# Attention with one more whole-array product per pair of heads in the narrow key blocks

## The chip, the cores and the metric

The kernel runs on one core of a Trainium2 chip. The time is the device time of that core in microseconds (us). The kernel before took 4295.83 us, the median of three runs (4293.31 to 4297.06).

## The reference

Two layers are computed for a batch of 2 sequences of 1024 tokens with 512 features. The change is in the attention of the first:

```python
q = (x @ Wq.T + bq).reshape(b, l, h, hd).transpose(0, 2, 1, 3)      # k and v alike; h = 32, hd = 16
scores = jnp.einsum('bhqd,bhkd->bhqk', q, k) / math.sqrt(hd)
causal = jnp.tril(jnp.ones((l, l), bool))
scores = jnp.where(causal, scores, -jnp.inf)
att = jax.nn.softmax(scores, axis=-1)
out = jnp.einsum('bhqk,bhkd->bhqd', att, v)
out = out.transpose(0, 2, 1, 3).reshape(b, l, d)
return out @ Wo.T + bo
...
x = x + _layernorm(_L0_attn_ref(_layernorm(x, axis=-1), ...), axis=-1)
x = x + _layernorm(_L0_ffn_ref(...), axis=-1)       # low-rank weight factors, silu
x = x + _layernorm(_L1_attn_ref(...), axis=-1)      # a state-space (Mamba) layer
x = x + _layernorm(_L1_ffn_ref(...), axis=-1)
```

## The kernel before, in words

A loop over the two batches runs every layer in turn. Each engine has its own program, and all follow one list, `ORDER`, made by `attention_order()`, so the order of work is written out by hand. Semaphores join the engines.

Attention works on eight groups of four heads, `t` = 0 to 7, here called quads. Queries and keys of a head are stacked as high and low parts in 48 rows (`ROWS`), with two rows more for the row maxima. An even quad has its rows from partition 0 on and an odd quad from partition 64 on.

A quad has twelve steps (`STEPS`), here called blocks 0 to 11. A block is one half `s` of the queries (512 of them) against one block `j` of 128 keys. Blocks 0 to 3 are the first half and blocks 4 to 11 the second. Since the attention is causal, blocks 1, 2, 3 and 9, 10, 11 are narrow: `lo` is 128, 256 and 384, and only 384, 256 or 128 queries are left. The other six blocks have 512.

In each block TensorE makes, for each of the four heads, a score product (L652) into `bank[h]`, and between them "pieces" (L628): the score products of the next quad with queries and keys exchanged, from which VectorE (DVE) takes the row maxima (L1237 with the mask, L1242 without). The pieces use a ring of three banks (4, 5, 7), and TensorE waits for `ring_free` before each. After the score products come the value products of the block before (`values`, L671), four heads side by side in the columns of the array. ScalarE (ACT) takes the exponential of two heads at once (L948, 384 of them), and TensorE waits for `exp_done[h // 2]` before it writes these two banks again. GpSimd (POOL) masks the diagonal block (L1608). The value products wait for that. The last block of a half ends in a copy `ot` on DVE (L1264), which is turned by four transposes (L681, "turn") in block 1 of the next quad and in block 7. Quad 7 has no pieces, because no quad follows it.

The query and key projections of later quads (L492, L493, L494: products over all 128 rows and columns) stand in blocks 1, 3, 5 and 7 of quads 1 and 3, twelve of them at a time. `xhi`, the input of the layer in its rounded form, stays in place until the attention has ended.

Of the kernel before, what the change touches and what calls it, by code (L numbers as in the profile page):

```python
# [24 lines left out]
P = 128  # L25
TT = L // P
KT = D // P
HALF = 512
# [35 lines left out]
def build(nc, x, w_attn, qk_bias, bv, bo, w_ffn0, lr0, lr0_const, w_ffn1,  # L64
          w_mamba, w_dt, conv_par, dt_bias, a_log, d_skip, out):
    ctx = ExitStack()
    with ctx:
        def sb(name, shape, dt=F32, stack=ctx):
            return stack.enter_context(nc.sbuf_tensor(name, shape, dt))
# [5 lines left out]
        bank = [banks[:, i, :] for i in range(8)]  # L75
# [4 lines left out]
        xhi = sb("xhi", [P, KT, L], F32R)  # L80
# [406 lines left out]
        def _(pe):  # L487
# [8 lines left out]
            def tokens(dst, i, w_hi, w_lo, cols=None):  # L496

                tok = slice(i * P, (i + 1) * P)
                for kt in range(KT):
                    r = three(dst, lambda k: xhi[:, k, tok], lambda k: xlo[:, k, tok],  # L500
                              lambda k: w_hi[:, k, :], lambda k: w_lo[:, k, :], kt, kt == 0, kt == KT - 1)
                return r

            def features(dst, w_hi, w_lo, s):

                tok = slice(s * HALF, (s + 1) * HALF)
                for kt in range(KT):
                    r = three(dst, lambda k: w_hi[:, k * P:(k + 1) * P], lambda k: w_lo[:, k * P:(k + 1) * P],
                              lambda k: xhi[:, k, tok], lambda k: xlo[:, k, tok], kt, kt == 0, kt == KT - 1)
                return r  # L510
# [85 lines left out]
            with pe.Fori(0, B) as b:  # L596
# [5 lines left out]
                for what, *arg in ORDER:  # L602
                    if what == "proj":
                        f, use = arg
                        which = use // 2
                        if use == 0:
                            pe.wait_ge(wqk_ready, b * 8 + 2 * f + 2)
                        if ring >= 3:
                            pe.wait_ge(ring_free, b * RING + ring - 2)
                        features(bank[RING_BANKS[ring % 3]][:], wqk_hi[:, which, :], wqk_lo[:, which, :], use % 2  # L610
                                 ).then_inc(ring_done, 1)
                        ring += 1
                    elif what == "values_in":
                        i, = arg
                        if i == 0:
                            pe.wait_ge(wv_ready, b + 1)
                        pe.wait_ge(ring_free, b * RING + ring - 2)
                        tokens(bank[RING_BANKS[ring % 3]][:], i, wv_hi, wv_lo).then_inc(ring_done, 1)
                        ring += 1
                    elif what == "piece":  # L620
                        t, n = arg
                        h, i, s, cols, _ = PIECES[n]
                        base, buf = 64 * (t % 2), t // 2 % 2
                        if n == 0:
                            pe.wait_ge(stacked[t % 2], (b * (NQ // 2) + t // 2 + 1) * STACKED)
                        pe.wait_ge(ring_free, b * RING + ring - 2)
                        dst = bank[RING_BANKS[ring % 3]]
                        r = pe.matmul(dst[:, 0:cols], stack_q[buf][base:base + ROWS, h, i * P:(i + 1) * P],  # L628
                                      stack_k[buf][base:base + ROWS, h, s * HALF:s * HALF + cols],
                                      start=True, stop=True)  # L630
                        r.then_inc(ring_done, 1)
                        ring += 1
                    elif what == "maxima":
                        t, = arg
                        pe.wait_ge(mx_ready, b * NQ + t + 1)
                        pe.wait_ge(ring_free, b * RING + ring - 2)
                        pe.transpose(bank[RING_BANKS[ring % 3]][0:QUAD * TT, 0:P], mx[:, 0, :], ident[:]
                                     ).then_inc(ring_done, 1)
                        ring += 1
                    elif what == "score":  # L640
                        t, n, h = arg
                        s, j = STEPS[n]
                        lo = max(j * P - s * HALF, 0)
                        base, buf = 64 * (t % 2), t // 2 % 2
                        it = b * (NQ * NS) + (t * NS + n)
                        if n == 0 and h == 0 and t % 2 == 0 and t < 4:
                            pe.wait_ge(ones_rows, b * (16 * 8) + 16 * 4 * (t // 2 + 1))
                        if n == 0 and h == 0:
                            pe.wait_ge(mt_in, START + (b * NQ + t + 1) * 32)
                        if h % 2 == 0:  # L650
                            pe.wait_ge(exp_done[h // 2], START + it)
                        r = pe.matmul(bank[h][:, 0:HALF - lo],  # L652
                                      stack_k[buf][base:base + ROWS + 2, h, j * P:(j + 1) * P],
                                      stack_q[buf][base:base + ROWS + 2, h, s * HALF + lo:(s + 1) * HALF],
                                      start=True, stop=True)
                        if h % 2:
                            r.then_inc(st_done[h // 2], 1)
                    elif what == "values":
                        t, n = arg
                        s, j = STEPS[n]  # L660
                        lo = max(j * P - s * HALF, 0)
                        it = b * (NQ * NS) + (t * NS + n)
                        if j == 0:
                            pe.wait_ge(ot_ready, START + b * (2 * NQ) + 2 * t + s)
                        for p in range(2):
                            if j * P >= s * HALF:
                                pe.wait_ge(masked[p], b * (NQ * TT) + (t * TT + j + 1))
                            else:
                                pe.wait_ge(exp_done[p], START + it + 1)
                        for h in range(QUAD):  # L670
                            r = pe.matmul(bank[6][32 * h:32 * h + VW, lo:HALF], V[:, j, QUAD * t + h, :],  # L671
                                          probs[n % 2][:, h, 0:HALF - lo], start=j == 0,
                                          stop=j == CPH * (s + 1) - 1, skip_group_check=True,
                                          tile_position=(0, 32 * h))
                        r.then_inc(pv_done, 1)
                    elif what == "turn":
                        t, s = arg
                        pe.wait_ge(ot_ready, START + b * (2 * NQ) + 2 * t + s + 1)
                        pe.wait_ge(ring_free, b * RING + ring - 2)
                        for k in range(CPH):  # L680
                            r = pe.transpose(bank[RING_BANKS[ring % 3]][:, k * P:(k + 1) * P], ot[:, k * P:(k + 1) * P], ident[:])  # L681
                        r.then_inc(ring_done, 1)
                        ring += 1
# [1104 lines left out]
```

## Time and profile before

| | us |
|---|---|
| median of the runs | 4295.83 |
| the profiled execution, its own time | 4294.83 |
| its span, from the first to the last instruction | 4293.1 |
| attention of the first batch, block 0 of quad 0 to the last value products | 347.27 |
| mean granted clock of TensorE over the span | 0.907 |

The clock is given as a share of full speed: 1.00 is 2.4 GHz and 0.50 is 1.2 GHz. A mean between them is a mixture of the two levels. In a row of the timeline the start of one product and the start of the next tell what the first one costs. The duration includes a pipeline that overlaps the next.

### The profile page before, as it was taken

How to read it: one execution, taken by the hardware profiler on the slowest of the kernel's cores; microseconds unless marked ns; L12 is line 12 of the kernel's file. 1: busy time of each engine (PE TensorE's matmuls, PEld its weight loads, DVE VectorE, ACT ScalarE, POOL GpSimd, SP SyncE). 2: the span in 40 equal slices, each digit the busy share in tenths (PEclk: the TensorE clock that was granted, in tenths of full speed). 3: DMA queues.
4: the chain of work that ended last, by engine and by line, in shares of the span. 5: the costliest groups of instructions: out<-in, count | busy, mean ns of one | idle time of the engine just before them, and what ended most of it. 6: DMA issues, size and time to landing. Idle time of an engine off the chain costs nothing.

```text
span 4293.1 us, 61464 instructions
## 1 busy us (share of the span) xinstructions
PE 3861.4 (90%) x18056; PEld 2813.5 (66%) x18056; DVE 2711.2 (63%) x5034; ACT 1695.2 (39%) x3538; POOL 1880.8 (44%) x2017
## 2 busy tenths in 40 slices
PE   7899799689999999979878896996899999999797
PEld 4444478567777777757654444885677777777576
DVE  3567445577777777764435673555777777777644
ACT  1344411355545555541113444113555555555411
POOL 1111344355555655654311113443555556655542
PEclk8677899899999999989977767998999999999899
DMA  3221011011100111001032210110101001110010
GB/s 73 36 36 31 24 51 45 22 33 30 32 20 25 34 32 29 22 15 45 35 81 36 36 32 29 46 45 22 35 28 32 20 25 34 32 29 22 15 52 35
DMA packets 81456, 145.59 MB, mean 34 GB/s; under 512 B 16392, under 2 KB 18520, under 8 KB 81264
## 3 DMA queue, kind: packets, MB, share of 16 engines
q1 hardware_dynamic: 81264, 143.28, 12.9%
q8 instruction: 90, 1.47, 0.1%
q14 instruction: 102, 0.84, 0.1%
HBM read 113.08 MB, written 4.19 MB: 27 GB/s over the span
## 4 chain that ended last, share of the span: by engine, by line
PE 69%; issue 11%; DVE 7%; ACT 4%; POOL 3%; DVEq 2%; POOLq 2%; DMA 1%; SPq 1%; ACTq 0%
PE banks L492 15%; PE banks L493 14%; PE banks L494 14%; PE banks L832 4%; PE banks L671 4%; PE banks L652 3%; PE banks L628 3%; PE banks L825 2%; PE banks L845 2%; DVE conv L1344 2%; DVEq L1347 1%; PE banks L767 1%; PE banks L768 1%; POOL X L1509 1%; ACT conv L1005 1%
## 5 line engine op out<-in xcount | busy, mean ns | idle before, releaser
L1344 DVE SCALAR_TENSOR_TENSOR conv<-banks,cpar,conv 128x509 f32<-128x509 f32 (+2 forms) x576 | 428.2, 744 | 115.3 <-ACT conv L1005 100.9
L948 ACT ACTIVATE probs<-banks 128x1024 f32<-128x1024 f32 (+3 forms) x384 | 297.7, 810 | 309.4 <-PE banks L652 308.9
L1172 DVE TENSOR_TENSOR Y<-banks,Y 128x512 f32<-128x512 f32 x400 | 276.1, 691 | 188.1 <-PE banks L494 187.9
L1608 POOL TENSOR_SCALAR_AFFINE_SELECT probs<-probs 128x256 f32<-128x256 f32 x256 | 104.2, 408 | 645.8 <-ACT probs L948 645.5
L628 PE MATMUL banks<-stack_k,stack_q 48*128 48x512 f32 (+3 forms) x768 | 331.7, 502 | 59.3 <-DVEq L1218 19.8
L1672 POOL TENSOR_TENSOR state<-state,gt 128x512 f32<-128x512 f32 x112 | 133.5, 1192 | 500.4 <-PE banks L825 500.4
L492 PE MATMUL banks<-xhi,f_hi 128*128 128x512 f32 x800 | 322.6, 403 | 3.5 <-DVE xlo L1143 3.5
L492 PE MATMUL banks<-xhi,wx_hi 128*128 128x512 f32 x768 | 312.0, 406 | 14.4 <-DVE conv L1344 14.4
L493 PE MATMUL banks<-xhi,f_lo 128*128 128x512 f32 x800 | 319.9, 400 | 0.0
L494 PE MATMUL banks<-xlo,f_hi 128*128 128x512 f32 x800 | 319.4, 399 | 0.0
L494 PE MATMUL banks<-xlo,wx_hi 128*128 128x512 f32 x768 | 306.0, 398 | 0.0
L493 PE MATMUL banks<-xhi,wx_lo 128*128 128x512 f32 x768 | 306.0, 398 | 0.0
L1237 DVE CUSTOM_DVE_ANT_0 banks<-banks,mask_qk 128x128 f32<-128x128 f32 (+3 forms) x512 | 248.1, 500 | 72.7 <-PE banks L628 59.4
L832 PEld LDWEIGHTS banks<-xdt,decay 128*128 128x128 f32 x2048 | 248.5, 192 | 65.2 <-issue 65.2
L652 PE MATMUL banks<-stack_q,stack_k 50*128 50x512 f32 (+3 forms) x768 | 274.7, 459 | 5.2 <-ACT probs L948 2.9
L628 PEld LDWEIGHTS banks<-stack_k,stack_q 48*128 48x128 f32 x768 | 163.0, 235 | 157.9 <-DVE mx L1242 51.1
L492 PE MATMUL banks<-wg_hi,xhi 128*128 128x512 f32 x512 | 222.3, 434 | 45.5 <-DVE conv L1344 42.2
L652 PEld LDWEIGHTS banks<-stack_q,stack_k 50*128 50x128 f32 x768 | 157.0, 232 | 155.5 <-issue 116.8
L832 PE MATMUL banks<-xdt,decay 128*128 128x64 f32 x2048 | 242.7, 272 | 2.4 <-DVE decay L1363 2.4
L910 ACT CAST h_hi<-hf 128x512 fp32r<-128x512 f32 x100 | 62.2, 622 | 441.0 <-DVE hf L1161 441.0
L518 PE MATMUL banks<-ident,xn 128*128 128x128 f32 x256 | 66.5, 426 | 188.1 <-ACT xn L892 165.3
L1076 ACT ACTIVATE yv<-banks,gt 128x64 f32<-128x64 f32 x1024 | 223.8, 332 | 24.8 <-PE banks L825 24.8
(209 smaller groups left out, 10185.0 us busy)
## 6 DMA issues: line engine op xcount, KB each, us to landing
m_raw<-in_w_mamba SPq DMA_DIRECT2D x224, 256.0 KB, 2.6
f_raw<-in_w_ffn SPq DMA_DIRECT2D x50, 768.0 KB, 4.5
stack_q<-part_hi SPq DMA_DIRECT2D x128, 64.0 KB, 2.4
stack_k<-part_hi SPq DMA_DIRECT2D x128, 64.0 KB, 2.5
X<-in_x SPq DMA_DIRECT2D x4, 1024.0 KB, 6.5
wqk_raw<-in_w_attn SPq DMA_DIRECT2D x8, 512.0 KB, 3.5
stack_q<-part_lo SPq DMA_DIRECT2D x64, 64.0 KB, 2.4
stack_k<-part_lo SPq DMA_DIRECT2D x64, 64.0 KB, 2.5
```

Source lines behind the costliest of these rows:

```text
L492: pe.matmul(dst, a_hi(kt), w_hi(kt), start=first, stop=False)
L493: pe.matmul(dst, a_lo(kt), w_hi(kt), start=False, stop=False)
L494: return pe.matmul(dst, a_hi(kt), w_lo(kt), start=False, stop=last)
L628: r = pe.matmul(dst[:, 0:cols], stack_q[buf][base:base + ROWS, h, i * P:(i + 1) * P], stack_k[buf][base:base + ROWS, h, s * HALF:s * HALF ...
L652: r = pe.matmul(bank[h][:, 0:HALF - lo], stack_k[buf][base:base + ROWS + 2, h, j * P:(j + 1) * P], stack_q[buf][base:base + ROWS + 2, h, s ...
L671: r = pe.matmul(bank[6][32 * h:32 * h + VW, lo:HALF], V[:, j, QUAD * t + h, :], probs[n % 2][:, h, 0:HALF - lo], start=j == 0, stop=j == C ...
L832: r = pe.matmul(bank[7][:, h * MP:(h + 1) * MP], decay[:, h, :], xdt[:, h * MP:(h + 1) * MP], start=True, stop=True, skip_group_check=True)
L948: act.activation(probs[n % 2][:, 2 * p:2 * p + 2, 0:w], banks[:, 2 * p:2 * p + 2, 0:w], ACT.Exp, scale=1.0 / HD ** 0.5).then_inc(exp_done[ ...
L1076: r = act.activation(yv[:, own], bank[6][:, own], ACT.Identity, scale=gt[:, EC, c, h:h + 1])
L1172: dve.tensor_tensor(Y[:, i, :], bank[6 + i % 2], Y[:, i, :], ALU.add).then_inc(f["dn_used"], 1)
L1237: dve.tensor_tensor_reduce(out=src, in0=src, in1=mask_qk[:, HALF - cols:HALF], scale=1.0, scalar=NEG, op0=ALU.add, op1=ALU.max, accum_out= ...
L1344: r = dve.scalar_tensor_tensor(out=rest, in0=src[:, 0:HALF - lag], scalar=cpar[:, o:o + 1], in1=rest, op0=ALU.mult, op1=ALU.add)
```

## The change

In a narrow block a product over the whole array, 128 rows and 128 columns by 512, is issued before the scores of heads 0 and 2. Its operands are two slices of `xhi`. It writes all of `bank[h]`, and the score product of that head overwrites it. Nothing reads its result.

```diff
                         if h % 2 == 0:
                             pe.wait_ge(exp_done[h // 2], START + it)
+                        if lo and h % 2 == 0:
+                            pe.matmul(bank[h][:], xhi[:, 0, 0:P], xhi[:, 0, 0:HALF], start=True, stop=True)
                         r = pe.matmul(bank[h][:, 0:HALF - lo],
                                       stack_k[buf][base:base + ROWS + 2, h, j * P:(j + 1) * P],
                                       stack_q[buf][base:base + ROWS + 2, h, s * HALF + lo:(s + 1) * HALF],
                                       start=True, stop=True)
```

In TensorE's program before, block 11 of quad 3 (128 queries left) up to its first value products reads as follows. `stack_q, stack_k` are scores and `stack_k, stack_q` are pieces.

```order
L651 REGISTER_ALU
L652 MATMUL banks<-stack_q,stack_k 128x128
L626 REGISTER_ALU
L628 MATMUL banks<-stack_k,stack_q 128x384
L652 MATMUL banks<-stack_q,stack_k 128x128
L626 REGISTER_ALU
L628 MATMUL banks<-stack_k,stack_q 128x512
L652 MATMUL banks<-stack_q,stack_k 128x128
```

The same place now. L653 is the new line, and the lines behind it have moved by two.

```order
L651 REGISTER_ALU
L653 MATMUL banks<-xhi 128x512
L654 MATMUL banks<-stack_q,stack_k 128x128
L626 REGISTER_ALU
L628 MATMUL banks<-stack_k,stack_q 128x384
L654 MATMUL banks<-stack_q,stack_k 128x128
L626 REGISTER_ALU
L628 MATMUL banks<-stack_k,stack_q 128x512
L653 MATMUL banks<-xhi 128x512
L654 MATMUL banks<-stack_q,stack_k 128x128
```

The first new product stands ahead of the first score product, the second between a piece and the third score product. Each takes over the wait for `exp_done`. There are 96 of them in the program of a batch, 192 in all. Nothing else on TensorE moves, and the other engines' programs are as they were.

## Rows read from the trace of the kernel before

**Rows 1.** The page: busy time of the engines, and TensorE's clock in 40 slices.

```profile
PE 3861.4 (90%) x18056; PEld 2813.5 (66%) x18056; DVE 2711.2 (63%) x5034; ACT 1695.2 (39%) x3538; POOL 1880.8 (44%) x2017
...
PEclk8677899899999999989977767998999999999899
```

**Rows 2.** Windows, with their columns: the first batch's attention, and 26 us of it.

```profile
core 0: us, PE busy (x) PEld busy (x) DVE busy (x) ACT busy (x) POOL busy (x), PEclk, DMA share, GB/s
127.23:474.50 347.27, 322.68 (x1645) 149.45 (x1645) 204.42 (x626) 154.04 (x200) 65.33 (x134) 0.74 0.20 36
370.00:396.00 26.00, 25.93 (x113) 10.82 (x114) 15.96 (x52) 9.91 (x13) 2.04 (x5) 0.50 0.00 1
```

**Rows 3.** Timeline of TensorE: start, us, engine, line, product; quad 4 to quad 5.

```profile
405.98 1.19 PE L671 MATMUL banks<-probs,V 128*17 128x256 f32 x16
407.11 0.49 PE L652 MATMUL banks<-stack_q,stack_k 50*128 50x512 f32 x1
...
408.95 0.44 PE L652 MATMUL banks<-stack_q,stack_k 50*128 50x384 f32 x1
...
411.09 1.91 PE L671 MATMUL banks<-probs,V 128*17 128x512 f32 x8
```

**Rows 4.** Windows: blocks 1 to 3 of quads 0, 1, 2, 3, 5 and 7.

```profile
129.56:141.46 11.90, 11.82 (x52) 4.54 (x52) 8.46 (x26) 4.45 (x7) 3.27 (x8) 0.50 0.70 106
169.91:195.67 25.76, 22.33 (x79) 11.92 (x80) 9.86 (x29) 4.97 (x8) 6.63 (x10) 0.60 0.00 1
230.38:241.98 11.60, 10.76 (x55) 4.20 (x54) 9.12 (x28) 4.34 (x7) 3.27 (x8) 0.74 0.68 102
271.67:294.92 23.25, 19.99 (x79) 10.19 (x79) 9.91 (x29) 4.98 (x8) 6.63 (x10) 0.71 0.00 1
367.56:380.68 13.12, 13.01 (x55) 4.95 (x54) 9.25 (x28) 4.34 (x7) 3.27 (x8) 0.56 0.00 1
449.54:457.09 7.55, 6.97 (x41) 3.04 (x41) 0.68 (x2) 4.12 (x7) 2.89 (x8) 0.77 0.27 96
```

**Rows 5.** Windows: blocks 4 to 8 of quads 0, 2, 4, 5 and 7.

```profile
141.46:160.10 18.64, 18.55 (x88) 8.33 (x85) 11.55 (x38) 9.69 (x10) 0.41 (x1) 0.57 0.61 99
241.98:261.74 19.76, 19.76 (x89) 8.98 (x86) 11.72 (x38) 9.69 (x10) 0.82 (x2) 0.50 0.60 98
341.19:357.93 16.74, 16.65 (x88) 7.30 (x84) 11.46 (x38) 9.69 (x10) 0.41 (x1) 0.68 0.63 103
380.68:399.30 18.62, 18.52 (x89) 8.27 (x85) 11.55 (x38) 9.69 (x10) 0.41 (x1) 0.58 0.00 1
457.09:468.60 11.51, 11.01 (x68) 4.25 (x64) 1.37 (x3) 9.02 (x10) 6.95 (x4) 1.00 0.00 0
```

**Rows 6.** Windows: blocks 9 to 11 of quad 4, and of quad 7 nearly to its end.

```profile
399.30:407.11 7.81, 7.07 (x59) 3.48 (x56) 6.02 (x20) 3.48 (x6) 2.86 (x7) 1.00 0.03 6
468.60:473.80 5.20, 4.89 (x40) 2.10 (x36) 0.00 (x0) 3.86 (x7) 2.74 (x8) 1.00 0.00 0
```

**Rows 7.** Timeline of TensorE: projection products at both clocks, then the scores.

```profile
303.47 0.63 PE L494 MATMUL banks<-xlo,wqk_hi 128*128 128x512 f32 x1
303.90 0.56 PE L492 MATMUL banks<-xhi,wqk_hi 128*128 128x512 f32 x1
...
305.70 0.40 PE L493 MATMUL banks<-xhi,wqk_lo 128*128 128x512 f32 x1
305.93 0.39 PE L494 MATMUL banks<-xlo,wqk_hi 128*128 128x512 f32 x1
306.25 0.50 PE L652 MATMUL banks<-stack_q,stack_k 50*128 50x512 f32 x1
...
306.59 0.62 PE L652 MATMUL banks<-stack_q,stack_k 50*128 50x512 f32 x2
```

**Rows 8.** Timeline of TensorE: pieces that wait for VectorE, in blocks 9 and 11.

```profile
400.58 0.50 PE L628 MATMUL banks<-stack_k,stack_q 48*128 48x512 f32 x1 [0.30 <-DVE mx L1242]
...
405.73 0.18 PEld L628 LDWEIGHTS banks<-stack_k,stack_q 48*128 48x128 f32 x1 [0.38 <-DVE mx L1237]
```

## The prediction, as put on record before the changed kernel ran

> **What bounds the kernel now.** I read the page first. TensorE is busy for 90% of the span, more than any other engine, and the row of its clock shows two dips. They lie in slices 2 to 6 and 22 to 25, where the two batches do their attention [rows 1]. Next I read the windows. The attention of the first batch takes 347.27 us at a mean clock of 0.74, with TensorE busy for 93% of it and VectorE for 59% [rows 2]. The second row says more: in 26 us TensorE is busy for 25.93 and the clock is 0.50 all along. So the clock is low where the engine is not idle at all. What it does there are score products and pieces of 50 and 48 rows and value products, with turns in between. The stretches at 1.00 follow the projections or a turn.
>
> The reader should then look at where the clock falls. In quad 4 it is 1.00 in blocks 9 to 11 [rows 6]. Then a double set of value products ends at 407.2 (405.98 plus 1.19), and until 411.09 there is nothing but scores and pieces: block 0 and then block 1 [rows 3]. The clock falls in that stretch. In nearly all quads the fall comes at this place. It rises again in block 1 or 2 in some quads (mean clock of blocks 1 to 3: 0.74 in quad 2, and quad 4 is like it) and in others only in block 7, when the turn is made (0.56 in quad 5, and quad 6 is like it) [rows 4]. Blocks 4 to 8 are mostly at 0.50: 18.64, 19.76 and 18.62 us, and 16.74 at 0.68 in quad 4, against 11.51 in quad 7, which has no pieces [rows 5].
>
> At the high clock the bound is another one. In blocks 9 to 11 of quad 4 VectorE is busy for 6.02 of 7.81 us and TensorE for 7.07 [rows 6], and pieces wait 0.30 and 0.38 us for the maxima [rows 8]. In blocks 1 to 3 VectorE needs 9.25 us at whatever clock [rows 4]. That is the floor there.
>
> **The change, part by part.** It adds 192 products: 2 in each of 6 blocks, 8 quads, 2 batches. It removes and moves nothing. Each takes over a wait that the score product had, so behind it in TensorE's queue stand that score product and all else of the block. ScalarE waits for them, and after it POOL's mask and the value products.
>
> *The price of one.* Inside a train of whole-array products one costs 0.23 us at the high clock (305.70 to 305.93) and 0.43 at the low one (303.47 to 303.90) [rows 7]. But these stand alone among products of another shape. After the last of a train the first score product comes 0.32 us later and the next pair another 0.34, where the plain spacing is 0.23 to 0.24: some 0.19 more for going over [rows 7]. I take 0.42 at the high clock. The lower end is 0.23, and nothing where all is covered. At the low clock I take 0.60, with 0.43 and 0.80 as the ends, since there the same detour costs up to twice as much. The Trainium skill (TensorEngine Tiling (Array Packing), Key Properties) says that changing the tiling mode drains TensorE. The trace agrees as far as the 0.19 us go. Without that rule the price would be 0.23 and the term of blocks 9 to 11 about half.
>
> *Blocks 9 to 11*, which run at 1.00 already. Nothing can be gained there. Six products of 0.42 are 2.5 us per quad. TensorE's idle 0.74 us (7.81 less 7.07) and the wait for the maxima hide about 1.0 of it [rows 6, 8], so 1.5 us remain in quads 0 to 6 of both batches: 14 × 1.5 = 21. In quad 7 there is no VectorE work to hide behind, the blocks take 5.20 us with TensorE busy for 4.89 [rows 6], and I count 2.3 for each: 4.6. Together **+25 us**. The ends are 5 (all covered) and 35.
>
> *Blocks 1 to 3.* The two products of block 1 fall into the stretch of rows 3, and those of blocks 9 to 11 move block 0 later by 1.5 us against the points at which the clock is set. Projections, which are products of the same kind, hold or restore the clock in quads 1 and 3. So I expect that some falls do not come, and that after others the clock is back by the turn in block 1. A quad without projections can go three ways. Without a fall the blocks cost VectorE's 9.25 plus 1.5 as above: 10.7 us. With a fall and an early rise they cost 12. Staying low they cost 13.1 plus six times 0.60: 16.7. I weigh these 0.5, 0.35 and 0.15, which gives 12.1. Against before that is −1.0 in quads 5 and 6 and +0.5 in quads 2 and 4 (11.60) [rows 4]. Quad 0 starts at the low clock and has no turn: 11.9 becomes 12.9. Quads 1 and 3 took 25.76 at clock 0.60 and 23.25 at 0.71, so 0.11 of clock is worth 2.5 us [rows 4]. With the clock at 0.8 and 0.85, and 0.9 for the products, they come to 22 and 21: −3.8 and −2.3. Quad 7, with 7.55 and no VectorE cover, pays 2.5 and gets 1.2 back: +1.3. The sum is −2.0 + 1.0 + 1.0 − 6.1 + 1.3 = −4.8 per batch, so **−10 us**. The ends are −36 (no falls: 9 to 18 per batch, see below) and +58 (96 × 0.60).
>
> *Blocks 4 to 8.* They get no product. When the clock is high at the end of block 3 it may last into block 4 or 5 before it falls. A block costs 4.0 us low and 2.8 high (18.62 for five, the last of them at the high clock; 7.81 for three narrow ones) [rows 5, 6]. Half a block saved in five quads of each batch is 0.6 × 10: **−6 us**. The ends are 0 and −44.
>
> The sum is 25 − 10 − 6 = +9 us on the profiled execution's 4294.83, so 4303.8. The median of the runs lies 1.0 higher, so I predict **4305 us**. A measurement of this kernel can tell a change of 0.2% (8.6 us) from none, so the forecast sits just at that bound.
>
> **The rivals.**
>
> *The clock is held through blocks 0 to 3 in every quad.* For it speaks that whole-array products do keep the clock in quads 1 and 3. Against it speaks that block 0, where the bare stretch begins, gets none, and that two products are little beside twelve. Blocks 1 to 3 would take 10.7 in five quads and 19, 18.5 and 8.3 in quads 1, 3 and 7: 99.3 against 117.7 before, −18 per batch. With +25 and −6 that gives 4295.83 − 17 = 4279.
>
> *It is then held through blocks 4 to 8 too.* They would take 5 × 2.8 = 14 us instead of 18.64, 19.76, 16.74 and twice 18.6: −22 per batch. Quad 7 runs these blocks at 1.00 throughout [rows 5], and quads 1 and 3 do it in part. Against it: block 4 has nothing but the shortest value products (128 queries) between scores and pieces, as barren a stretch as block 0. The time would be 4295.83 + 25 − 36 − 44 = 4241.
>
> *Slower: bought at the low clock.* The mechanism is that the two products of a block are too few to move a rise or a fall, and blocks 1 to 3 pay the price at 0.50. The price is 0.60 × 96 = 58 us, less what projections give back in quads 1 and 3, with 25 in blocks 9 to 11 on top: 4295.83 + 45 + 25 = 4366 at the full price, and 4340 if VectorE still hides a part. It decides if the mean clock of blocks 1 to 3 in quads 5 and 6 stays below about 0.7. For it speaks that TensorE is never idle there, so every product shows in full.
>
> *TensorE's busy time decides the clock.* The Trainium skill (TensorE: Matmul & The Clock Gate, Part 1) says that the clock follows how busy the engine has recently been. Rows 2 contradict the plain reading of that: busy for 25.93 of 26 us at 0.50. As a mechanism of this kernel it would leave the clock as it is, since the engine is busy already. The time is then that of the slower rival, and its chance is in that one's.
>
> *The products cost nothing and do nothing*, because waits for VectorE and ScalarE hide them. Idle time of TensorE is 25 us in the first attention (347.27 less 322.68) [rows 2], which is no more than a part of what they take. That would be 4298.
>
> **How the numbers follow.** Forecast 0.45, with its own range 4285 to 4325. The clock held in blocks 0 to 3: 0.18. Held further: 0.10. Bought at the low clock: 0.20. Nothing: 0.07. The likeliest gives 4305. The range of 8 in 10 leaves out most of the second rival below and the dear half of the third above: 4256 to 4350. Slower by over 0.2% is half of the forecast (0.22), the third rival (0.20) and a bit more: 0.45. Faster is the first two rivals and a sixth of the forecast: 0.35. The rest is 0.20.
>
> **What would show it.** In the windows of the changed kernel, blocks 9 to 11 of quads 0 to 6 should be 1.5 us longer at clock 1.00. Blocks 1 to 3 of quads 5 and 6 should have a mean clock of about 0.8 and last 12 us. The new line should have 192 products. A product should delay its neighbours by 0.4 us. The forecast is wrong if blocks 4 to 8 come down from 18.6 to near 14 us (then the clock is held), if blocks 1 to 3 grow by more than 2 us (then it was bought at the low clock), or if the narrow blocks at 1.00 grow by less than 0.5 us (then the price is hidden).

## The result, and the profile after

The changed kernel takes 4338.26 us (median of nine runs, 4325.41 to 4361.07) against 4297.06 us of the kernel before in the same comparison (nine runs, 4290.15 to 4315.62). The ratio is 1.0103, with a 95% interval of 1.0079 to 1.0127: slower by 1.0%. The direction was forecast and the time lies in the range, but the loss is 41 us where I had forecast 9.

The profiled execution took 4358.16 us, near the upper end of its kernel's runs, and its span is 63.2 us longer than before. That is 22 us more than the medians differ, so the two traces show more of a loss than the kernels usually have. The page, answering to [rows 1], shows the 192 products more, TensorE busy for 68 us more, and the other engines as they were.

```profile
PE 3929.1 (90%) x18248; PEld 2839.6 (65%) x18248; DVE 2711.8 (62%) x5034; ACT 1699.0 (39%) x3538; POOL 1877.9 (43%) x2017
```

The windows of the changed kernel follow, the ones that answer to [rows 2, 4]: the attention of the first batch, blocks 1 to 3 of its quads 0, 1, 2, 3, 5 and 7, and the attention of the second batch.

```profile
core 0: us, PE busy (x) PEld busy (x) DVE busy (x) ACT busy (x) POOL busy (x), PEclk, DMA share, GB/s
128.99:499.92 370.93, 348.69 (x1733) 158.96 (x1733) 204.31 (x626) 156.14 (x200) 64.94 (x134) 0.79 0.19 33
132.04:146.80 14.76, 14.76 (x57) 5.43 (x57) 7.97 (x25) 3.72 (x7) 2.85 (x7) 0.50 0.65 106
177.41:204.34 26.93, 22.64 (x84) 12.37 (x83) 9.50 (x29) 4.70 (x8) 6.29 (x10) 0.68 0.00 1
241.33:251.16 9.83, 9.63 (x61) 4.29 (x60) 8.05 (x27) 4.03 (x7) 2.94 (x8) 1.00 0.63 103
289.48:310.93 21.45, 18.27 (x84) 9.37 (x84) 9.05 (x27) 4.41 (x8) 6.21 (x9) 0.85 0.00 1
382.96:394.28 11.32, 11.25 (x62) 4.85 (x61) 7.94 (x27) 4.01 (x7) 2.90 (x8) 0.85 0.01 2
461.40:474.56 13.16, 13.16 (x47) 5.64 (x46) 0.68 (x2) 3.73 (x7) 2.78 (x7) 0.50 0.03 13
...
2301.89:2675.19 373.30, 350.67 (x1729) 159.73 (x1733) 204.57 (x626) 155.83 (x199) 64.76 (x133) 0.79 0.19 33
```

The mean clock of the first attention rose from 0.74 to 0.79, and the attention is 24 us longer all the same. Quads 2 and 5 got what was hoped for: 11.60 us became 9.83 and 13.12 became 11.32. Quad 7 went from 7.55 at 0.77 to 13.16 at 0.50.

Next, to be read against [rows 5, 6], blocks 4 to 8 of quads 2, 4 and 7, and blocks 9 to 11 of quads 2 and 4:

```profile
251.16:271.17 20.01, 19.48 (x90) 8.08 (x86) 12.30 (x40) 9.62 (x10) 0.81 (x2) 0.59 0.60 96
357.23:371.42 14.19, 13.48 (x89) 5.53 (x85) 11.89 (x40) 9.62 (x10) 0.79 (x3) 1.00 0.64 103
474.56:492.51 17.95, 17.95 (x70) 7.11 (x66) 1.37 (x3) 9.53 (x10) 6.88 (x4) 0.56 0.00 1
271.17:286.42 15.25, 15.25 (x62) 6.61 (x62) 6.50 (x20) 3.59 (x6) 2.44 (x6) 0.50 0.02 4
371.42:380.69 9.27, 8.80 (x62) 4.23 (x62) 6.07 (x20) 3.58 (x6) 2.48 (x7) 1.00 0.26 46
```

In quad 4 the clock was held through blocks 4 to 8: 14.19 us against 16.74 [rows 5]. In quad 2 it fell early in these blocks and did not come back within the quad, and blocks 9 to 11 took 15.25 us at 0.50, where before they took 8.09 at 0.90. In quad 7 blocks 4 to 8 took 17.95 against 11.51.

Such windows over all quads of both batches account for the attention (us, sum of both batches):

| | before | after | change | forecast |
|---|---|---|---|---|
| blocks 9 to 11 | 121.1 | 158.8 | +37.7 | +25 |
| blocks 0 to 3 | 267.1 | 275.9 | +8.8 | −10 |
| blocks 4 to 8 | 300.3 | 309.5 | +9.3 | −6 |
| of all these, quad 7 | 53.3 | 84.3 | +31.0 | +7 |

That is 55.8 of the 63.2 us. The rest lies around the attentions. The first product of block 1 is issued before that block's first score and so falls into the window of block 0, and that of block 9 into the window of blocks 4 to 8. Blocks 1 to 3 alone are 1 us shorter than before, and block 0 is 10 us longer over the sixteen quads.

### The profile page after: what moved, and what is told of

It reads as the page before. It is cut to its first block, busy times and chain, and to the rows that moved or that the text cites. A ratio compares the mean times of both kernels' runs of the same rounds, so it can differ in the third digit from the quotient of the medians.

```text
span 4356.3 us, 61848 instructions
## 1 busy us (share of the span) xinstructions
PE 3929.1 (90%) x18248; PEld 2839.6 (65%) x18248; DVE 2711.8 (62%) x5034; ACT 1699.0 (39%) x3538; POOL 1877.9 (43%) x2017
## 3 DMA queue, kind: packets, MB, share of 16 engines
q1 hardware_dynamic: 81264, 143.28, 12.6%
## 4 chain that ended last, share of the span: by engine, by line
PE 71%; issue 11%; DVE 7%; ACT 4%; POOL 3%; DVEq 2%; POOLq 2%; SPq 1%; DMA 0%; ACTq 0%
PE banks L492 15%; PE banks L493 14%; PE banks L494 14%; PE banks L834 4%; PE banks L673 4%; PE banks L654 4%; PE banks L628 3%; PE banks L827 2%; PE banks L653 2%; PE banks L847 2%; DVE conv L1346 2%; DVEq L1349 1%; PE banks L769 1%; PE banks L770 1%; POOL X L1511 1%
## 5 line engine op out<-in xcount | busy, mean ns | idle before, releaser
L628 PE MATMUL banks<-stack_k,stack_q 48*128 48x512 f32 (+3 forms) x768 | 306.3, 464 | 52.4 <-DVEq L1220 18.7
L1492 POOL TENSOR_SCALAR f_hi<-f_raw 128x512 fp32r<-128x512 f32 x150 | 95.8, 639 | 312.9 <-PE banks L494 293.8
```

## The experiments

In each kernel only the condition or the body of the two new lines differs. The kernel before was timed beside each group on the same chip, so the ratio is what counts, and not the distance to a time that I expected: its own median was 4298.83, 4302.77 and 4307.06 us in the three groups. As a measure of the clock I also give its mean over blocks 1 to 3 of quads 4, 5 and 6 of both batches, six windows of one profiled execution each. One trace is one sample: in several of them the two batches have the same pattern nearly window for window. It is 0.58 in the kernel before and 0.88 in the changed one.

**Blocks 1 to 3 only.**

```diff
-                        if lo and h % 2 == 0:
+                        if lo and s == 0 and h % 2 == 0:
```

> The added products stand only in blocks 1 to 3 (96 of the 192), the other narrow blocks are as before. My theory (the products act on TensorE's clock, and where the clock is high they cost 0.4 us each): blocks 9 to 11 with block 0 shrink from 11.5 to 9.7 us per quad, blocks 1 to 3 of quads 4 to 6 stay at 10 to 12 us, the time is about 4308 (4290 to 4325). The rival (the products only take TensorE time, the clock follows other things): half of the loss goes, 4317, and the clock in blocks 1 to 3 of quads 5 and 6 is as before, 0.54 to 0.56.

Measured: 4306.09 us (12 runs), ratio 1.0023 (1.0006 to 1.0040). The clock measure is 0.94. The trace is of the fastest of the twelve (4283.64), so it shows the best case. The rows are blocks 1 to 3 of quad 6, blocks 9 to 11 of quad 5 and, in the second batch, blocks 4 to 8 of quad 5.

```profile
408.31:418.00 9.69, 9.66 (x62) 4.27 (x61) 7.91 (x27) 4.01 (x7) 2.91 (x8) 1.00 0.00 0
...
398.25:406.04 7.79, 7.06 (x60) 3.48 (x56) 6.00 (x20) 3.48 (x6) 2.84 (x7) 1.00 0.03 8
...
2522.24:2536.00 13.76, 13.04 (x88) 5.34 (x84) 11.88 (x40) 9.63 (x10) 0.43 (x2) 1.00 0.00 1
```

As expected, the price in blocks 9 to 11 is gone (7.79 against 9.27 us) and the clock is held in the first half. Quads 4, 5 and 6 of the second batch ran from block 1 to block 8 at 1.00, 23.4 us each, where the same three took 28.8 to 29.5 before. The rival's clock of 0.54 to 0.56 did not come. Without the other half of the products three quarters of the changed kernel's loss are gone.

**Blocks 9 to 11 only.**

```diff
-                        if lo and h % 2 == 0:
+                        if lo and s == 1 and h % 2 == 0:
```

> The added products stand only in blocks 9 to 11 (96 of the 192). My theory: these blocks run at the high clock already, so nothing is gained; they pay 1.9 us per quad, 30 us in all, and block 0 only comes later against the points at which the clock is set; blocks 1 to 3 are as before, 13 us in quads 5 and 6. The time is 4325 (4310 to 4340). The rival (price only, half of it): 4317.

Measured: 4335.27 us (6 runs), ratio 1.0095 (1.0076 to 1.0115), clock measure 0.61. The rows are blocks 4 to 8 of quad 7 in the first batch, and blocks 1 to 3 and 9 to 11 of quad 5 in the second.

```profile
458.56:478.25 19.69, 19.69 (x69) 7.49 (x65) 1.38 (x3) 9.69 (x10) 7.30 (x5) 0.50 0.00 1
2543.15:2556.14 12.99, 12.92 (x54) 5.21 (x54) 8.88 (x28) 4.45 (x7) 3.25 (x8) 0.50 0.00 1
2572.16:2581.41 9.25, 8.78 (x61) 4.24 (x61) 6.07 (x20) 3.59 (x6) 2.47 (x7) 1.00 0.03 7
```

This half alone brings nearly the whole loss, 0.95% of 1.03%. Blocks 9 to 11 are 28 us longer than before over both batches (9 of them in quad 7), with no return, and quad 7 was at the low clock though its blocks 1 to 3 had no products.

**No products in quad 7.**

```diff
-                        if lo and h % 2 == 0:
+                        if lo and t + 1 < NQ and h % 2 == 0:
```

> The changed kernel without the added products in quad 7 (168 are left). My theory: the loss in quad 7 (blocks 1 to 8 went from 19 to 31 us in the first batch, at the low clock) is partly the products there; without them blocks 1 to 8 go back to about 20 us, and the time falls by 25 to 4313. The rival (price only): 24 products by 0.42 us, so 4328. A third case: quad 7 stays at the low clock since the clock depends on when it starts, then about 4325 with blocks 4 to 8 of quad 7 still near 18 us.

Measured: 4337.08 us (10 runs), ratio 1.0071 (1.0047 to 1.0095). Four runs lie at 4308.5 to 4313.1 and six at 4336.3 to 4341.6, with none between. The trace is of one at 4310. Its rows are blocks 1 to 3 and 4 to 8 of quad 7, first in batch one and then in batch two.

```profile
452.05:461.37 9.32, 9.12 (x41) 3.82 (x41) 0.68 (x2) 4.22 (x7) 3.18 (x8) 0.52 0.14 52
461.37:478.53 17.16, 17.16 (x68) 6.68 (x65) 1.38 (x3) 9.10 (x10) 6.62 (x4) 0.56 0.00 1
2608.10:2615.67 7.57, 6.99 (x40) 3.06 (x40) 0.68 (x2) 4.12 (x7) 2.87 (x8) 0.77 0.16 60
2615.67:2627.18 11.51, 11.00 (x68) 4.26 (x64) 1.37 (x3) 9.00 (x10) 6.91 (x4) 1.00 0.01 1
```

The third case holds for the first batch. With not one product in it, quad 7 took 7.4 us longer there in these blocks than in the second batch of the same execution, plain instructions against plain instructions. My 4313 was wrong as a median. The two traces also give the price at the low clock: the changed kernel's blocks 1 to 3 (13.16 us) have five whole products more than these 9.32, so 0.77 each where nothing covers them. In quad 0, also at the low clock, five products made 11.90 us into 14.76, which is 0.57 each.

**The score product twice instead of a whole-array product.**

```diff
-                            pe.matmul(bank[h][:], xhi[:, 0, 0:P], xhi[:, 0, 0:HALF], start=True, stop=True)
+                            pe.matmul(bank[h][:], stack_k[buf][base:base + ROWS + 2, h, j * P:(j + 1) * P],
+                                      stack_q[buf][base:base + ROWS + 2, h, s * HALF:(s + 1) * HALF],
+                                      start=True, stop=True)
```

> Instead of the product over the whole array the score product itself is made once more, 50 rows by 128 columns by 512, same places and number, so TensorE streams the same number of elements with no change of the array's shape. My theory (it is the whole array that holds the clock): the clock is as in the kernel before, 0.54 to 0.56 in blocks 1 to 3 of quads 5 and 6, which last 13.1 plus 6 times 0.43 = 15.7 us; the time is 4340 (4325 to 4360). The rival (any product holds it): clock of blocks 1 to 3 of quads 4 to 6 at 0.85 to 1.0 and 10 to 11.5 us as in the changed kernel, time 4320 as the price is smaller.

Measured: 4327.16 us (6 runs), ratio 1.0069 (1.0053 to 1.0086), clock measure 0.72. The rows are blocks 9 to 11 of quad 5, blocks 1 to 3 of quad 6 (both of the first batch), and blocks 1 to 3 of quad 4 in the second.

```profile
403.98:412.31 8.33, 7.93 (x62) 4.29 (x59) 6.05 (x20) 3.48 (x6) 2.57 (x7) 1.00 0.03 8
414.49:427.87 13.38, 13.31 (x61) 6.28 (x59) 8.98 (x28) 4.11 (x7) 3.02 (x8) 0.51 0.01 1
2493.65:2503.00 9.35, 8.56 (x60) 4.16 (x57) 7.88 (x27) 4.12 (x7) 3.03 (x8) 1.00 0.62 103
```

The price is 0.5 us for blocks 9 to 11 instead of 1.5. The array's shape does not change, and some of the products run beside a piece: the one that starts at 403.64 us has a piece starting at 403.65. How much of the difference each of these makes was not separated. The clock is between the two theories: as without products in two quads of the first batch, held in one of the second. One trace can't decide it, for reasons that the later runs show. What stands is that 50 rows held it in fewer places than 128 did in any of the five traces with two whole-array products in each of blocks 1 to 3 only or of all narrow blocks there (0.72 against 0.88 to 0.96). The time lost is less all the same, 0.7% against the changed kernel's 1.0%.

**Blocks 1 to 3 of quads 2, 4, 5 and 6.**

```diff
-                        if lo and h % 2 == 0:
+                        if lo and s == 0 and t in (2, 4, 5, 6) and h % 2 == 0:
```

> The added products stand only in blocks 1 to 3 of quads 2, 4, 5 and 6 (48 of the 192). My theory: these are the places where they turn low clock into high and nothing else needs their time; against the version with products in blocks 1 to 3 of all quads (4306) quads 0, 3 and 7 save 3.6, 3.6 and 2.7 us per batch, so about 4286, faster than the kernel before by 0.3% (4270 to 4300). Blocks 4 to 8 of quads 4 to 6 at a clock of 0.9 to 1.0 and 14 to 15 us. The rival (the clock is a matter of chance and the products do not steer it): the clock of these quads is as in the kernel before, 0.5 to 0.7 in blocks 1 to 8, and the time is 4299 plus 48 by 0.5 = 4323.

Measured: 4289.59 us (12 runs, 4272.61 to 4310.03), ratio 0.9966 (0.9944 to 0.9989): the only version faster than the kernel before. The clock measure is 0.96. The rows are blocks 1 to 3 and 4 to 8 of quad 4, blocks 4 to 8 of quad 7, and in the second batch blocks 9 to 11 of quad 3.

```profile
327.93:337.59 9.66, 9.64 (x62) 4.27 (x61) 7.91 (x27) 4.01 (x7) 2.90 (x8) 1.00 0.64 105
337.59:351.36 13.77, 13.07 (x88) 5.34 (x84) 11.88 (x40) 9.63 (x10) 0.43 (x2) 1.00 0.60 98
436.95:454.30 17.35, 17.35 (x69) 6.80 (x65) 1.38 (x3) 9.10 (x10) 6.64 (x4) 0.56 0.00 1
2452.57:2464.29 11.72, 11.72 (x60) 5.70 (x56) 6.20 (x20) 3.47 (x6) 2.45 (x7) 0.50 0.12 20
```

The clock was up through blocks 1 to 8 in seven of the eight quads with products (mean 0.85 and more), and these eight are 36 us shorter than in the trace before. But 31 us of it are lost in the other quads of this trace. Quad 7 lies low in both batches (+20 us), and quad 3 of the second batch fell after its projections and took 11.72 us for blocks that take 7.8 (+10 for the quad). The eighth, quad 4 of the second batch, comes right behind it and starts at the low clock.

**Two products in blocks 0, 1, 4 and 5.**

```diff
-                        if lo and h % 2 == 0:
+                        if n in (0, 1, 4, 5) and t + 1 < NQ and h % 2 == 0:
```

> The added products (two per block) stand in blocks 0, 1, 4 and 5 of quads 0 to 6, where the clock is seen to fall, instead of the narrow blocks (112 products). My theory (a fall comes where scores and pieces run for long with hardly any value products): the clock stays at 1.00 from block 4 on in most quads without projections, blocks 4 to 8 take 14 to 15 us with part of the products hidden behind VectorE, 9 to 11 are 7.8; the time is 4290 (4270 to 4310). The rival (place does not matter, only the number of products): about as the changed kernel scaled to 112 of 192 products, 4320, with low stretches in blocks 4 to 8 as before.

Measured: 4350.73 us (6 runs), ratio 1.0095 (1.0066 to 1.0124), clock measure 0.79: my expectation of 4290 failed by 60 us. The rows are blocks 1 to 3 and 4 to 8 of quad 4, and 4 to 8 of quad 5.

```profile
342.22:356.54 14.32, 14.25 (x57) 5.41 (x57) 8.68 (x27) 3.99 (x7) 2.85 (x7) 0.50 0.63 102
356.54:374.61 18.07, 17.98 (x88) 6.92 (x87) 11.61 (x37) 9.91 (x10) 0.41 (x1) 0.72 0.31 52
394.72:408.88 14.16, 13.97 (x90) 5.58 (x89) 11.56 (x39) 9.91 (x10) 0.41 (x1) 1.00 0.00 1
```

Quad 5 went as I thought and most others did not: blocks 4 to 8 were at a clock of 0.55 to 0.72 in five of six windows of quads 4 to 6, and the products there were paid at the low clock. So filling the places where the fall is seen is not enough. That blocks 2 and 3, which have little of everything, have to be filled too is my reading. This run left 6 to 11 bare as well, and can't tell them apart.

**Two products in every block of quads 0 to 6.**

```diff
-                        if lo and h % 2 == 0:
+                        if t + 1 < NQ and h % 2 == 0:
```

> Two added products in every block of quads 0 to 6 (168). If the clock can be held by such products at all, it is 1.00 nearly throughout quads 2, 4, 5 and 6 once it has risen. The price is 24 products per quad by 0.42 us, partly hidden: quads 4 to 6 take 36 to 38 us each against 41 before and 33.5 with products in blocks 1 to 3 and a held clock. Time 4320 (4300 to 4345). The rival (they only take time): 4299 + 168 by 0.45 = 4375.

Measured: 4335.28 us (10 runs), ratio 1.0071 (1.0049 to 1.0093), clock measure 0.92. The rows are blocks 4 to 8 of quad 4 and block 0 and blocks 1 to 3 of quad 5.

```profile
362.81:378.65 15.84, 15.84 (x96) 6.25 (x95) 11.82 (x39) 10.25 (x10) 0.54 (x2) 1.00 0.60 96
388.64:392.38 3.74, 3.74 (x11) 1.57 (x10) 1.95 (x6) 1.64 (x2) 0.41 (x1) 0.50 0.02 4
392.38:404.99 12.61, 12.60 (x61) 5.34 (x61) 8.55 (x26) 3.99 (x7) 2.84 (x7) 0.77 0.00 1
```

Blocks 4 to 8 ran at 1.00 in quads 1 to 6 of both batches, and TensorE is then busy for 15.84 of 15.84 us. So the clock can be held there, and 2.1 us a quad is what it costs against 13.77. Even so the clock still fell ahead of block 0 of quad 5 in both batches, and with a price in every block the kernel is 0.7% slower. The rival's 4375 is excluded.

**The products at 128 columns instead of 512.**

```diff
-                            pe.matmul(bank[h][:], xhi[:, 0, 0:P], xhi[:, 0, 0:HALF], start=True, stop=True)
+                            pe.matmul(bank[h][:, 0:P], xhi[:, 0, 0:P], xhi[:, 0, 0:P], start=True, stop=True)
```

> The changed kernel with each added product only 128 columns long instead of 512, so that its own stream is a quarter and the change of shape stays. It measures the price's two parts: I took 0.23 us for the stream and 0.19 for going over. Then a product and what follows it takes about 0.26 us at the high clock against 0.42, blocks 9 to 11 are 8.3 to 8.5 us (7.8 before, 9.27 in the changed kernel). My theory for the clock: a quarter of the whole-array work holds it less, blocks 1 to 3 of quads 5 and 6 at 0.55 to 0.7 and 13 us. Time 4320 (4305 to 4335). The rival (the count of products, not their length, holds the clock): 0.85 and 11 us there.

Measured: 4368.27 us (4 runs), ratio 1.0146 (1.0106 to 1.0185): the slowest of all. The clock measure is 0.50, below that of the kernel before. The timeline of TensorE in block 11 of quad 0 first (start, us, product), then the windows of blocks 1 to 3 of quad 5, 9 to 11 of quad 0 and 9 to 11 of quad 3.

```profile
168.29 0.33 PE L653 MATMUL banks<-xhi 128*128 128x128 f32 x1
168.54 0.32 PE L654 MATMUL banks<-stack_q,stack_k 50*128 50x128 f32 x1
```

```profile
388.02:402.04 14.02, 14.02 (x60) 6.20 (x60) 9.20 (x27) 4.05 (x7) 2.96 (x8) 0.50 0.01 2
162.12:170.69 8.57, 8.10 (x61) 4.28 (x60) 6.04 (x20) 3.59 (x6) 2.66 (x7) 1.00 0.07 13
330.53:344.18 13.65, 13.65 (x61) 6.61 (x61) 6.45 (x20) 3.58 (x6) 2.44 (x6) 0.50 0.22 35
```

The price came out as expected: 0.25 us from the product to the next score, so going over costs 0.2 and the columns the rest. The time did not. A short product is nearly all detour. It stretches the quad and gives the clock nothing that this trace shows: quads 4 to 6 of both batches lay at 0.50 in all three blocks. The same count of products of 512 columns had 0.88 there, so it is not the count that holds the clock.

**Quad 7 added to quads 2, 4, 5 and 6.**

```diff
-                        if lo and h % 2 == 0:
+                        if lo and s == 0 and t in (2, 4, 5, 6, 7) and h % 2 == 0:
```

> The version with products in blocks 1 to 3 of quads 2, 4, 5 and 6 (4290) with quad 7 added to them (60 products). Without products quad 7 lay at the low clock in both batches of that version's trace (9.3 us for blocks 1 to 3, 17.4 and 19.0 for 4 to 8); with products in all quads' blocks 1 to 3 it took 9.8 and 11.5. My theory: the products bring the clock back there, quad 7 saves 5 us a batch, the time is 4280 (4265 to 4292). The rival (quad 7's clock is luck of when it starts, the products only cost 2.7 us there): 4295.

Measured: 4317.11 us (12 runs), ratio 1.0004 (0.9983 to 1.0025), clock measure 0.88. Five runs lie at 4294 to 4297, six at 4316 to 4322 and one far off at 4478.74. The trace is of one of the five. Its rows are blocks 1 to 3 and 4 to 8 of quad 7 in batch one and in batch two.

```profile
442.42:455.50 13.08, 13.08 (x46) 5.56 (x45) 0.68 (x2) 4.01 (x7) 2.85 (x8) 0.50 0.12 41
455.50:474.47 18.97, 18.97 (x68) 7.21 (x65) 1.38 (x3) 9.69 (x10) 7.29 (x5) 0.50 0.00 1
2594.43:2604.29 9.86, 9.86 (x46) 4.43 (x45) 0.68 (x2) 3.72 (x7) 2.44 (x6) 0.73 0.16 60
2604.29:2615.80 11.51, 11.00 (x68) 4.26 (x65) 1.37 (x3) 9.00 (x10) 6.99 (x4) 1.00 0.01 1
```

The same six products with the same neighbours came with the high clock in one batch (0.73 in blocks 1 to 3 and 1.00 behind them) and the low one in the other. In quad 7 they steer nothing reliably, and my theory that they bring the clock back there has fallen.

**Blocks 9 to 11 of quad 6 only.**

```diff
-                        if lo and h % 2 == 0:
+                        if lo and s == 1 and t == 6 and h % 2 == 0:
```

> The kernel before with the added products only in blocks 9 to 11 of quad 6 (12 products in all), which run at the high clock. They delay block 0 of quad 7 by 1.5 us and do nothing else. My theory for the unforeseen part of the loss (quad 7 at the low clock is a matter of when its blocks 0 and 1 come, not of the products in it): quad 7's blocks 1 to 8 go from 19 to 26 or 28 us in one batch or both, for a price of only 3 us, so the time is 4299 + 3 + 14 = 4316. The rival (the products within quad 7 did it): quad 7 as before, 4302.

Measured: 4316.39 us (12 runs, 4293.94 to 4348.83), ratio 1.0020 (0.9994 to 1.0046): not told apart from no change. The rows are blocks 9 to 11 of quad 6, blocks 1 to 3 and 4 to 8 of quad 7, and blocks 9 to 11 of quad 1.

```profile
453.93:462.28 8.35, 7.77 (x56) 3.42 (x55) 3.17 (x9) 3.59 (x6) 2.48 (x7) 1.00 0.14 26
464.12:473.44 9.32, 9.31 (x41) 3.92 (x41) 0.68 (x2) 4.33 (x7) 3.19 (x8) 0.51 0.13 49
473.44:490.50 17.06, 17.06 (x69) 6.68 (x65) 1.38 (x3) 9.09 (x10) 6.62 (x4) 0.57 0.00 0
225.39:237.11 11.72, 11.72 (x59) 5.69 (x56) 6.21 (x20) 3.48 (x6) 2.46 (x7) 0.50 0.26 57
```

The trace is of one of the slowest of the twelve (4342.37). In it quad 7 lies low in both batches, as I expected (26.4 us for its blocks 1 to 8 against 19.1). But the last row takes away the proof. Quads 0 to 5 of this program are those of the kernel before, and quad 1's blocks 9 to 11 took 11.72 us at 0.50 where they took 7.79 at 1.00 before. So the pattern differs between two executions of the same instructions, and one trace each does not show that the shift did it. That the median is the 4316 I wrote down is luck: I meant 17 us above the kernel before, and it is 9 above that of its own chip.

The same holds earlier still. Quad 0 has no products in six of the programs: the kernel before, the one with quads 2, 4, 5 and 6, and the last four of this section. Its blocks 4 to 8 took 15.6, 16.7 or 18.6 us, and all three lengths occur in the first batches of these six traces, where no product has been issued yet. The draw begins there.

**One product per block, in quads 2, 4, 5, 6 and 7.**

```diff
-                        if lo and h % 2 == 0:
+                        if lo and s == 0 and t in (2, 4, 5, 6, 7) and h == 0:
```

> As the version with blocks 1 to 3 of quads 2, 4, 5, 6 and 7, but one product per block, before head 0, instead of two (30 products). It halves the price (blocks 1 to 3 at the high clock 9.4 us instead of 9.7, since VectorE is the floor) and shows if one is enough to hold the clock. My theory: it holds it in fewer quads, clock of blocks 1 to 3 of quads 4 to 6 about 0.8 instead of 1.0, 4288 (4272 to 4302). The rival (one is as good as two): 4274.

Measured: 4320.78 us (12 runs), ratio 1.0024 (1.0007 to 1.0040), clock measure 0.87. The row is blocks 4 to 8 of quad 2.

```profile
243.31:261.17 17.86, 17.77 (x89) 7.50 (x85) 12.23 (x40) 9.69 (x10) 0.41 (x1) 0.62 0.60 97
```

In blocks 1 to 3 one product did as well as two (0.87 against 0.88). In blocks 4 to 8 it did not: those of quads 2 and 6 are at 0.62 in both batches, where two products had 0.89 to 1.00. The intervals of the two versions' ratios overlap, so the times don't tell them apart.

**Two products in block 1 only, of the same quads.**

```diff
-                        if lo and h % 2 == 0:
+                        if n == 1 and t in (2, 4, 5, 6, 7) and h % 2 == 0:
```

> Two products in block 1 only, of quads 2, 4, 5, 6 and 7 (20 products). It tells whether it is block 1, where the fall comes, or the row of blocks 1 to 3 that has to be filled. My theory: the clock comes back in block 1 in more quads, but falls again in block 2 or 3 or at block 4 as in quads 2 and 4 of the kernel before, so blocks 4 to 8 stay at 16 to 18 us and the time is 4295 (4280 to 4305). The rival (block 1 is all that matters): 4275, with blocks 4 to 8 at 13.8.

Measured: 4314.05 us (12 runs), ratio 1.0011 (0.9997 to 1.0026), clock measure 0.76. The rows are blocks 1 to 3 and 4 to 8 of quad 4.

```profile
324.34:335.54 11.20, 10.47 (x58) 4.06 (x57) 8.64 (x28) 4.01 (x7) 2.93 (x8) 0.73 0.65 105
335.54:353.62 18.08, 17.98 (x89) 7.98 (x85) 11.56 (x38) 9.70 (x10) 0.41 (x1) 0.60 0.61 100
```

As expected, blocks 4 to 8 are as before: 17.4 us on average over quads 4 to 6 of both batches, against 17.1 before and 14.8 with products in blocks 1, 2 and 3 of the same quads. Blocks 1 to 3 themselves got what the six products gave them, 11.1 us against 12.7 before and 11.0 with six. So it is the products in blocks 2 and 3 that carry the clock on into block 4, as far as one trace of each shows. Whether block 3 alone would do was not run.

## Why the prediction was right or wrong

**What bounds the kernel** was read rightly in the main: TensorE is slow in the attention although it is busy. The floor that I gave blocks 1 to 3 was wrong. I took 9.25 us of VectorE "at whatever clock" from windows at the low clock and put 1.5 on top for the case without a fall, 10.7. In the windows without a fall these blocks took 9.7, with VectorE busy for 7.9 and TensorE for nearly all of it. There TensorE with its added products is the bound, and not VectorE.

**The price of one product** was right at the high clock. Two rows of the changed kernel's timeline show a product in block 11 of quad 7:

```profile
498.29 0.50 PE L653 MATMUL banks<-xhi 128*128 128x512 f32 x1
498.72 0.44 PE L654 MATMUL banks<-stack_q,stack_k 50*128 50x128 f32 x2
```

That is 0.43 us against 0.42 forecast, and the short products put the detour at 0.2 as read from [rows 7]. The Trainium skill (TensorEngine Tiling (Array Packing), Key Properties) says that a change of the tiling mode drains TensorE. These 0.2 us agree with it. At the low clock the price was 0.57 in quad 0 and 0.77 in quad 7 against 0.60 taken, inside the ends.

**Blocks 9 to 11**: 1.46 us a quad at the high clock (7.81 to 9.27), plus 0.43 for the first product of block 9, which falls into the window of blocks 4 to 8. That makes 1.9 where I had 1.5: my cover by VectorE was put too high by 0.4, or 6 us in all. Most of what the +37.7 lies above the forecast is another thing. In quad 2 of both batches these blocks ran at the low clock, 7.2 us more each, and so did those of quad 7 in the second. The sentence that failed is that they "run at 1.00 already".

**Blocks 1 to 3**: for quads 2, 4, 5 and 6 the direction held. I forecast 12.1 us, and the changed kernel's eight windows are between 9.7 and 12.6 with a mean of 10.7. The terms that came out too small are quad 0 (12.9 forecast, 14.8 measured, the low clock all through), quad 1 (22 forecast, 26.9 measured) and quad 7. In quad 1 the clock rose, but from 0.60 to 0.68 and not to 0.8, and that did not even pay for the products.

**Blocks 4 to 8**: the saving was there in quad 4 of both batches (−2.5 and −2.3) and in quad 6 of the first (−3.1), and was lost in quad 7 (+6.4 and +7.5).

**Quad 7** is the main miss: +31 us where I had 7, in two traces that differ by 22 us more than the medians do, so it may be less in a median run. I had taken its clock of the one trace before for a property of the kernel. It has no pieces, and at the low clock its blocks 1 to 8 take 26.5 us against 19.1 without a single product in it. The runs without products in quad 7 show that it falls without them too. What decides whether it falls is open: in eleven of the twelve experiments' traces it lay low in one batch or both (in eight of them in both), with and without products in quad 7. In the traces of the kernel before and of the version with blocks 1 to 3 only it did so in neither. Since two traces of like instructions differ, many traces of the kernel before would be needed to tell how often it falls there. The two clusters of runs in two of the experiments, with 23 and 28 us between their middles, suggest that such a loss comes whole or not at all; that quad 7 makes them was not shown.

**The rivals.** The clock held in blocks 0 to 3 and beyond was true in some quads and not in others. The dear rival, bought at the low clock, was true in quads 0 and 7. The measured time lies between my forecast and that rival. But the rival's own sign did not come: the mean clock of blocks 1 to 3 in quads 5 and 6 was 0.73 to 0.85, not below 0.7. So that the time lies in the range is owed to its width and not to the sum. Giving one theory to all quads was the weakness. That the clock follows TensorE's busy time is refuted once more: quad 7 of the changed kernel is busy for 13.16 of 13.16 us at 0.50.

## What to carry to other kernels

Products made only to hold the clock pay where the work around them would go at the low clock and the high clock is worth several times their price. Put elsewhere they lose: the same lines in blocks that mostly ran at the high clock already brought 36 us more, and in the quads where they helped they made the kernel 0.3% faster. Judge such a change by many runs and count the windows at each clock in more than one trace, since one trace's pattern is a draw. Make the products long, because most of a short one is the detour. Whole-array products held the clock in more places than those of 50 rows. These cost a third at the high clock and lost less when put everywhere, and they were not run in the right places only.

## What the runs showed of the hardware

- Two levels in one program: blocks 1 to 3 of quad 7, with the same six products and neighbours, took 9.86 us and 13.08 us in two batches of one execution.
- 35 runs of the kernel before on one chip spread from 4289.56 to 4325.30 us, far more than the 4 us of its first three. Nine runs of each kernel left an interval of 0.24% to either side, so my 0.2% was too fine a bound.
- With whole-array products of 128 columns the mean clock of the same blocks was no higher than with no products at all (0.50 against 0.58, one trace each).
- An added product of 50 rows costs a third of one over the whole array (0.5 against 1.5 us for six).
